# Two stacked window-attention blocks on one core: the bias and mask table moved from a TensorE product to a ScalarE copy, and the query and key products split into high and low parts

## What is computed

```python
h = roll(layernorm(x), (-3, -3)) cut into windows of 7x7 = 49 tokens
q, k, v = h @ qkv_w + qkv_b, per head
attn = softmax((q * hd**-0.5) @ k.T + rel_bias[head] + mask[window])
x = x + roll(windows_back(attn @ v @ proj_w + proj_b), (3, 3))
x = x + gelu(layernorm(x) @ fc1_w + fc1_b) @ fc2_w + fc2_b
```

## Time and profile before

| | |
|---|---|
| median of 3 runs | 7130.31 us |
| time of the profiled execution | 7130.83 us |
| its span in the trace | 7129.1 us |
| granted TensorE clock over the span | 0.997 |
| TensorE busy | 98% |
| VectorE, ScalarE, GpSimd busy | 71%, 66%, 63% |
| mean busy share of the 16 DMA engines | 0.18 |

### The profile page before, as it was taken

The page is one execution under the profiler, slowest core; times in us unless marked ns, Lnnn a source line. Parts: engine busy times, 40 slices in busy tenths (PEclk is TensorE's granted clock), DMA queues, the critical chain, the costliest instruction groups (busy, mean ns, idle before and its releaser), DMA issues.

```text
span 7129.1 us, 284978 instructions
## 1 busy us (share of the span) xinstructions
PE 6951.3 (98%) x98848; PEld 5895.1 (83%) x98848; DVE 5031.9 (71%) x18727; ACT 4674.0 (66%) x9220; POOL 4523.6 (63%) x4612
## 2 busy tenths in 40 slices
PE   6999999999999999999999999999999999999999
PEld 5888888888888888888888888888888888888887
DVE  5777777777777777777777777777777777777775
ACT  3666666666666666666666666666666666666665
POOL 3666666666666666666666666666666666666665
PEclk9999999999999999999999999999999999999999
DMA  1111111111111111111111111111111111111111
GB/s 49 47 46 46 46 46 45 46 45 46 45 46 45 46 45 46 45 47 45 47 45 47 45 47 45 47 44 47 44 48 44 48 44 48 43 48 43 48 43 37
DMA packets 604563, 325.43 MB, mean 46 GB/s; under 512 B 450142, under 2 KB 604128, under 8 KB 604320
## 3 DMA queue, kind: packets, MB, share of 16 engines
q1 hardware_dynamic: 604528, 324.96, 17.5%
HBM read 80.71 MB, written 38.54 MB: 17 GB/s over the span
## 4 chain that ended last, share of the span: by engine, by line
POOL 30%; PE 27%; issue 24%; DVE 17%; POOLq 1%; DVEq 0%; SPq 0%; DMA 0%; ACT 0%
POOL hid_sq L956 8%; POOL x_biased L947 7%; PE ps L422 5%; PE ps L526 5%; PE ps L430 5%; POOL hid_ss L958 4%; POOL rstd L967 4%; POOL rstdM L928 4%; PE ps_o L503 3%; PE ps L515 3%; POOL rstdA L928 3%; DVE x_next L890 3%; DVE bnA L801 2%; DVE bnM L801 2%; DVE o_norm L841 2%
## 5 line engine op out<-in xcount | busy, mean ns | idle before, releaser
L928 POOL TENSOR_TENSOR rstdM<-var_epsM,minus_half 98x4 f32<-98x4 f32 x512 | 515.4, 1007 | 1292.6 <-DVE var_epsM L809 1292.6
L830 DVE TENSOR_TENSOR shifted<-ps,negmax 113x392 f32<-113x392 f32 x2048 | 1161.4, 567 | 213.2
L669 ACT ACTIVATE probsT<-ps 98x392 f32<-98x392 f32 x2048 | 952.3, 491 | 431.3 <-PE ps L483 419.7
L928 POOL TENSOR_TENSOR rstdA<-var_epsA,minus_half 98x4 f32<-98x4 f32 x512 | 518.0, 1012 | 1100.0 <-DVE var_epsA L809 1100.0
L826 DVE TENSOR_REDUCE negmax<-ps 113x8 f32<-113x392 f32 x2048 | 1142.7, 558 | 56.4 <-PE ps L471 28.1
L686 ACT ACTIVATE hid<-ps,bfc 128x392 f32<-128x392 f32 x1536 | 873.0, 587 | 416.3 <-PE ps L542 399.2
L662 ACT ACTIVATE probs<-shifted 113x392 f32<-113x392 f32 x2048 | 997.7, 526 | 23.5 <-DVE shifted L830 15.2
L483 PE MATMUL ps<-ident,probs 113*98 113x113 f32 x8192 | 990.7, 264 | 9.2 <-ACT probs L662 7.7
L503 PEld LDWEIGHTS ps_o<-vM,probsT 98*49 98x49 f32 x32768 | 793.8, 125 | 195.6 <-DVE o_norm L841 128.2
L503 PE MATMUL ps_o<-vM,probsT 98*49 98x50 f32 (+1 forms) x32768 | 851.4, 201 | 78.9 <-DVE o_norm L841 78.7
L483 PEld LDWEIGHTS ps<-ident,probs 113*98 113x98 f32 x8192 | 800.9, 129 | 52.8 <-ACT probs L662 9.6
(11 more groups left out here) (99 smaller groups left out, 15077.7 us busy)
## 6 DMA issues: line engine op xcount, KB each, us to landing
kM<-kT SPq DMA_DIRECT2D x512, 85.8 KB
vM<-vA SPq DMA_DIRECT2D x1024, 41.3 KB
vM<-vA SPq DMA_DIRECT2D x1024, 38.3 KB
x_in<-in_x SPq DMA_DIRECT2D x256, 147.0 KB
x_again<-in_x SPq DMA_DIRECT2D x256, 147.0 KB
kM<-kT SPq DMA_DIRECT2D x1024, 36.8 KB
x_keep<-x_next SPq DMA_DIRECT2D x256, 147.0 KB
out_y<-y_out SPq DMA_DIRECT2D x256, 147.0 KB
```

The costliest lines, as they stand in the source:

```text
L669: act.activation(probsT[:, unit_buffer(L, u), :, :, :], free(ps[bank_of[f"T{L}{u}"]][0:PT, 0:1], (SP, 4), (64, 2), (1, TOK)), ACT.Copy).th ...
L830: dve.tensor_tensor(shifted[:, buf, :].rearrange("p (h k) -> p h k", k=TOK), s, free(negmax[:, buf, 0:1], (1, 8), (0, TOK)), ALU.add).then ...
L928: pool.tensor_tensor(rstd[n][:, :], var_eps[n][:, :], minus_half[:, :], ALU.pow).then_inc(s_rstd[n], 1)
```

## The change

The table: `tleft`, `t_high`, `tlow` and the product L462 go. `table` becomes a plain float32 array of 113 rows that holds bias plus mask for every unit, and a new step of ScalarE, `seed`, copies a unit's part of it into the bank (8 a turn). The scores add onto what ScalarE wrote. For that the places of a bank must count as written by TensorE: only the first matmul of a group that fills a bank starts afresh, three groups are padded from 384 to 392 columns (`PAD` = 8, in `project` and block 1's `fc2`), all banks are filled once at the start, and `scores` of block 0 opens with one matmul of a single column that adds zero.

Queries and keys: `turned` of an A norm now makes two copies on ScalarE, `xqT_high` (float32r) and `xnT`; a new step of VectorE, `low_part_qk`, makes `xqT_low`; `q` and `k` are three float32r products each (`three`, which `fc1` uses too), and their high and low weights are made once at the start.

The orders of all five engines and `BANKS` are new, and LAST is 5: block 0's MLP now works on s2, block 1's attention from the scores on s3, its first MLP part on s4 and its last on s5. `turn` is the same instruction as `pe.transpose`, with other start and stop flags.

```diff
@@ scores @@
-                for u in units:
-                    if free_from := bank_free(x, f"sc{L}{u}"):
-                        pe.wait_ge(*free_from)
-                    if u == units[-1]:
-                        pe.wait_ge(s_qe[L], x.count(1, 1))
-                        pe.wait_ge(s_km[L], x.count(16 * VARIANTS[L], 16 * VARIANTS[L]))
-                    pe.matmul(ps[bank_of[f"sc{L}{u}"]][0:SP, 0:UNIT_COLS], tleft[:, :], table_of(x, L, u),
-                              start=True, stop=False, skip_group_check=True)
+                pe.wait_ge(s_qe[L], x.count(1, 1))
+                pe.wait_ge(s_km[L], x.count(16 * VARIANTS[L], 16 * VARIANTS[L]))
+                pe.wait_ge(s_sd[L], x.count(UNITS[L], units[-1] + 1))
+                if L == 0:
+
+                    pe.matmul(ps[bank_of["sc00"]][0:1, 0:1], ident[:, 1:2], ident[:, 0:1], start=False, stop=True, skip_group_check=True)
@@ scalar @@
+            def seed(x, L, u):
+
+                if x.exists(ns):
+                    if free_from := bank_free(x, f"sc{L}{u}"):
+                        act.wait_ge(*free_from)
+                    act.activation(ps[bank_of[f"sc{L}{u}"]][0:SP, 0:UNIT_COLS], table_of(x, L, u), ACT.Copy).then_inc(s_sd[L], 1)
@@ turned @@
+                    act.activation(xqT_high[L][0:C, :], g, ACT.Copy).then_inc(s_xh[L], 1)
                     act.activation(xnT[L][0:C, :], g, ACT.Copy).then_inc(s_xe[n], 1)
@@ tensor @@
+            def three(out, w_high, w_low, x_high, x_low, low_ready):
+
+                pe.matmul(out, w_high, x_high, start=True, stop=False)
+                pe.matmul(out, w_low, x_high, start=False, stop=False)
+                pe.wait_ge(*low_ready)
+                return pe.matmul(out, w_high, x_low, start=False, stop=True)
@@ q (k alike) @@
-                    pe.wait_ge(s_xe[f"A{L}"], x.count(1, 1))
+                    pe.wait_ge(s_xh[L], x.count(1, 1))
-                    pe.matmul(ps[bank_of[f"q{L}"]][0:QK[L], 0:ST], wqkv[L][:, 0:QK[L]], xnT[L][:, :], start=True, stop=True)\
-                      .then_inc(s_q[L], 1)
+                    three(ps[bank_of[f"q{L}"]][0:QK[L], 0:ST], wqk_high[L][:, 0:QK[L]], wqk_low[L][:, 0:QK[L]],
+                          xqT_high[L][:, :], xqT_low[L][:, :], (s_ql[L], x.count(1, 1))).then_inc(s_q[L], 1)
@@ vector @@
+            def low_part_qk(x, L):
+
+                if x.exists(ns):
+                    dve.wait_ge(s_xe[f"A{L}"], x.count(1, 1))
...
+                    dve.tensor_tensor(xqT_low[L][0:C, :], ps[bank_of[f"xtA{L}"]][0:C, 0:ST], xqT_high[L][0:C, :].bitcast(f32),
+                                      ALU.subtract).then_inc(s_ql[L], 1)
```

More of the change, by code:

```diff
@@ L45, in shape_constants @@
     k = {"ident": np.eye(128, dtype=np.float32)}
[L48 to L58, removed]
+    masks = []
     for last_row in (0, 1):
@@ L62, in shape_constants @@
                 first, pairs, _, heads = unit_place(L, u)
-                block = np.zeros((NREG, pairs, heads, TOK), np.float32)
+                block = np.zeros((SP, pairs, heads, TOK), np.float32)
                 for p in range(pairs):
[L65 to L73, removed]
+                    other_row = rr[:, None] != rr if last_row else np.zeros((TOK, TOK), bool)
+                    other = other_row | (rc[:, None] != rc) if first + p == PAIRS - 1 else other_row
+                    block[HALF[0]:HALF[0] + TOK, p] = -100.0 * other_row[:, None]
+                    block[HALF[1]:HALF[1] + TOK, p] = -100.0 * other[:, None]
+                masks.append(block.reshape(SP, -1))
+    k["mask"] = np.concatenate(masks, 1)
     return k
@@ L404, in _, with turn @@
             pe.wait_ge(s_brow, 32)
+            for bank in ps[:7]:
+                mm = pe.matmul(bank[:, 0:4 * SP], ident[:, :], free(ident[:, 0:1], (0, 4), (1, SP)), start=True, stop=True)
+            mm.then_inc(s_wps, 1)
+            def turn(out, x, first, last):
+                rows = x.ap[0][1]
+                return pe.matmul(out, x, ident[0:rows, 0:rows], start=first, stop=last, is_transpose=True, skip_group_check=True)
             def xT(x, n):
@@ L557, in fc2 @@
                     for c in range(HCH):
-                        w = wfc2[:, c, :] if L == 0 else par128[1][:, P128["fc2"] + C * c:P128["fc2"] + C * (c + 1)]
-                        mm = pe.matmul(g[0:PT, p * step:p * step + width], hid[L][:, c, t], w, start=(c == 0), stop=(c == HCH - 1))
+                        if L == 1 and p == PAIRS - 1 and c == HCH - 1:
+                            width = C + PAD
+                        w = wfc2[:, c, :] if L == 0 else par128[1][:, P128["fc2"] + C * c:P128["fc2"] + C * c + width]
+                        mm = pe.matmul(g[0:PT, p * step:p * step + width], hid[L][:, c, t], w, start=(p == c == 0), stop=(c == HCH - 1),
+                                       skip_group_check=True)
                     if L == 0:
@@ L654, in v_out, with table_of @@
                        .then_inc(s_ve[L], 1)
+            def table_of(x, L, u):
+                col = UNIT_COLS * unit_buffer(L, u)
+                if x.known:
+                    start = (1 if x.i - x.off >= last_row_from else 0) * NT + col
+                    return table[:, start:start + UNIT_COLS]
+                which = (x.i + (256 - last_row_from - x.off)) // 256
+                return table[:, bass.ds(which * NT + col, UNIT_COLS)]
+            def seed(x, L, u):
[3 more added lines that the diff above has]
+                    act.activation(ps[bank_of[f"sc{L}{u}"]][0:SP, 0:UNIT_COLS], table_of(x, L, u), ACT.Copy).then_inc(s_sd[L], 1)
             def exps(x, L, u):
@@ L690, in body @@
                 s0, s1, s2, s3, s4 = Strip(i, 0), Strip(i, 1), Strip(i, 2), Strip(i, 3), Strip(i, 4)
+                gelu(s2, 0, 0)
+                gelu(s2, 0, 1)
+                gelu(s2, 0, 2)
+                seed(s3, 1, 4)
+                seed(s3, 1, 5)
+                exps(s3, 1, 0)
+                probsT_out(s3, 1, 0)
+                exps(s3, 1, 1)
+                exps(s1, 0, 0)
+                exps(s3, 1, 2)
+                turned(s0, "A0")
+                exps(s3, 1, 3)
+                exps(s3, 1, 4)
@@ L726, in _ @@
+                q_out(s0, 0)
+                k_out(s2, 1)
+                gelu(s4, 1, 0)
+                q_out(s2, 1)
+                gelu(s4, 1, 1)
+                seed(s2, 1, 0)
+                seed(s2, 1, 1)
+                seed(s2, 1, 2)
+                turned(s1, "M0")
+                v_out(s0, 0)
+                gelu(s4, 1, 2)
+                v_out(s2, 1)
+                seed(s2, 1, 3)
             iterate(act, body)
@@ L895, in body @@
             def body(i):
[L896 removed]
+                s0, s1, s2, s3, s4, s5 = Strip(i, 0), Strip(i, 1), Strip(i, 2), Strip(i, 3), Strip(i, 4), Strip(i, 5)
                 stats(s0, "A0")
+                low_part(s2, 0)
+                shift(s3, 1, 0)
+                shift(s3, 1, 1)
+                shift(s3, 1, 2)
+                stats(s4, "M1")
+                finish1(s5)
+                shift(s3, 1, 3)
+                shift(s3, 1, 4)
+                shift(s3, 1, 5)
                 third_stats(s2)
[L899 removed]
+                low_part_qk(s0, 0)
                 finish0(s2)
```

236 lines of the change are left out of this document (104 added, 132 removed), and 12 rows, old and new, of the table BANKS.

## The result

The changed kernel takes 7067.72 us, the median of 4 runs (7063.67 to 7070.04). The kernel before took 7129.89 in the same session. The ratio is 0.991, 95% interval 0.990 to 0.993: faster, by 0.9% instead of the 3.1% predicted.

What follows compares the result with a forecast made beforehand. The prediction took TensorE to bound the kernel, with a VectorE chain close behind; after the change, the keys' landing ends a 26.45 us turn. 256 turns (6771) plus 135 give a 6906 us span, time 6907 us, range 6690 to 7050.

Steps and rivals of the forecast that it cites:

- the turn: One pass of the steady loop, 256 in all: 26.45 us, ended by the landing of block 1's keys; chance 0.5.
- the walk: Step-by-step timing of a new turn across the engines: TensorE ready at 25.8 us, the keys there at 26.45.
- 135: Setup, filling and draining outside the 256 turns: 115 us as before plus 20 for the change.
- SyncE's three fixed issues: On SyncE's queue, load_residual, the next turn's load and block 1's key DMAs follow each other; keys there at 26.45 us.
- the 24.4 us of the walk: TensorE's work in a new turn if nothing waited: 26.5 - 1.85 - 0.4 + 0.1 us.
- the forecast's 26.5: TensorE's work in a 27.4 us turn of the kernel before, counted from group start to group start.
- The idle time ahead of attend of block 0: Expected sign on TensorE: an idle stretch of 0.3 us there, ended by o_norm.
- (1): The key DMAs are not last; shifts, ps_o and TensorE set a 25.8 us turn: 6690 to 6800 us; chance 0.23.
- (2): The order hides nearly everything and TensorE is the bound again: a 24.8 us turn, 6484 us; chance 0.06.
- (3): Smaller delays add on the same chain, up to 0.6 us: a 27.0 us turn, 7050 us; chance 0.13 up to 7115.
- (4): ScalarE's seeds make the kernel slower from 0.9 us each; at 1.0 us each the time is 7330 us; chance 0.05.
- no drain: ScalarE's table loads: 1.28 us each, without the skill's 1.38 us drain, which would add some 130 us to the forecast.

Runs made afterwards that it cites:

- e1: The changed kernel with its two 113-row start loads (bias table and mask) each cut into 112 rows and 1 row: 6927.1 us, 0.971 of the kernel before.
- e9: e1 plus one 64 KB DMA of ident, into a buffer nothing reads, ahead of block 1's key DMAs on SyncE: 7072.6 us, 0.991 of the kernel before.
- e12: e10 with finish1 ahead of the middle statistic (M1) on VectorE instead of behind it: 6921.3 us, 0.970 of the kernel before.
- e6: e1 with each seed made by ScalarE in four pieces of 98 columns: 7241.9 us, 1.015 of the kernel before.
- e10: e4 with one VectorE statistic, A0 of the next strip, moved behind the shift and low part of block (1,0): 6848.3 us, 0.960 of the kernel before.
- e4: e1 with SyncE's list reordered so that block 1's key DMAs follow block 0's at once: 6922.6 us, 0.971 of the kernel before.
- e3: e1 with SyncE's keep(s3) put ahead of block 1's key DMAs: 8763.5 us, 1.229 of the kernel before.
- e8: e4 with two VectorE statistics moved: A0 of the next strip behind normalise(1,0), M1 to the end of the turn before: 7059.3 us, 0.989 of the kernel before.

## Why the prediction was wrong in the sum and right in the turn

- **The step that failed** is a term of the sum: "One more turn of pipeline, a larger table to load and the matmuls that fill seven banks at the start come to it; bounded by nothing ... and by one turn and a half, 40 us, I take 20". It was 173 us. 138 of them (287.9 - 150.3) are the two loads with 113 rows; the other 35 are the rest of that sentence and lie inside its bounds. I gave the larger table no price of its own, and the bound of 40 us came from no row. Its bytes would not have found the miss: 1.6 MB more at the 239 GB/s of the start before are 7 us, and e1, with all the bytes, does wait only 6 us longer than the kernel before (28.9 to 22.8). What the walk lacked is that the loads of 98 rows became loads of 113, and that 113 rows go at 26 GB/s. With 135 replaced by 287.9 the same walk gives 7060 us, 0.1% from the measured time.
- The Trainium skill, DMA: Bandwidth & Descriptors, "Why a DMA increments its semaphore by 16 and not by 1", says that a DMA is spread over the largest number of engines up to 16 that divides the size of the slowest dimension of both its patterns: 113 is prime, so one engine; 106 gives two, 112 sixteen. The traces agree: a share of 0.06 and 26 GB/s with 113 rows, 0.12 and 53 GB/s between 40 and 50 us with 106. By that rule the prediction could have had the term.
- **The turn**, 26.45 predicted, 26.485 measured. The keys did end last and SyncE's three fixed issues stood in a row as walked; e9 shows that a delay of them is paid nearly whole. But it was not the forecast's clear margin. I had TensorE ready at 25.8 with 0.5 to 0.7 us of idle time; it was ready at 26.3, with 0.18 of wait and another chain, VectorE's statistic and low part, 0.12 behind. I had read VectorE as ready in time for the next turn and did not see the statistic that opens its turn. Since all three lay within 0.3 us of each other, the number came out right; that it did so to 0.04 us is partly luck.
- **TensorE's work** was more than the 24.4 us of the walk, which went by starts; its busy time, 25.72, is another measure and covers part of each wait. In the kernel before, attend of block 0 starts 0.57 us behind the matmul ahead of it, where that kind follow each other at 0.08, but only 0.32 shows as idle; so the forecast's 26.5 there does not contradict the 26.99 of busy time. By starts, the changed kernel loses about 0.48 ahead of 3503.99, 0.42 ahead of 3513.16, and 0.18 and 0.12 at the end of the turn, 1.2 in all, which leaves some 25.3 of work, an estimate: 0.9 over the walk. About 0.5 of it is what was not saved: by busy time the table products gave 1.49 instead of 1.85 and the split 0.25 instead of 0.4. The rest, 0.4 to 0.5, is work that the new order has more (by busy time, 26.99 - 1.49 - 0.25 = 25.25 against 25.72). Which handovers hold it was not tried.
- The idle time ahead of attend of block 0 was there (0.26 us), but ended by the turned probabilities, not by o_norm; e12 shows how near o_norm stands.
- **The rivals.** (1), TensorE setting the turn at 25.8, did not happen: TensorE arrived later and the keys held. (2) was out of reach, since work alone is about 25.3. (3), small delays, is where the time lay, but for a wrong reason: the turn had none of them. (4): a seed takes 0.49 us (mean 494 ns, two in 0.92), near the Exp of the earlier trace rows, but e6 shows that its threshold of 0.9 was too high and its mechanism not the one that bites: at 0.70 a seed the kernel is 1.5% slower than before, with ScalarE 85% busy, because TensorE waits for late seeds. (By the forecast's own sum 27.33 us a turn is also the point of no change, not that of 0.2% slower.) The table load took 1.28 us with the next Exp 0.01 us behind it, so no drain here either.
- What the change consists of, by e1's neighbours: the seeds 1.0 us a turn, the split 0.28, together 1.28, while the turn fell by 0.92. If the two add up, which no run tested, all the rest of the change, the new order above all, costs about 0.36 us a turn; e10's order gives 0.32 of that back.

## What to carry to other kernels

Look at the number of rows of every load that a change touches, and not at its bytes alone, at the start too: on a kernel of 7 ms two loads with a prime number of rows took away two thirds of the gain of a rebuilt loop, and cutting each in two brought it back. When several chains end within a few tenths of a microsecond, shortening one can give nothing (e4), and the second step the whole (e10); so look at the distance between two groups on the bounding engine and compare it with the smallest one seen, since the trace names a wait only when it is long. And before a step is moved ahead of others on a queue, find what it waits for itself: e3, e8 and e12 each moved a wait to a worse place.

## What was not expected of the hardware

- A load of 113 rows moves 26 GB/s with a busy share of 0.06, one of 106 rows 53 GB/s with 0.12; the same bytes as 112 rows and 1 let the first product start at 28.9 us instead of 169.5. Later loads in the same queue are held up at their issue too (80.58 us for two).
- A wait of 4.6 us in each turn brought TensorE's granted clock to 0.86 on the mean; the products behind it were 0.33 us apart instead of 0.18.
- ScalarE writes 113 x 392 float32 from SBUF into a bank in 494 ns and a quarter of it in 240 ns: by the two sizes, 240 - (494 - 240)/3 = 155 ns of a duration are fixed, an estimate. In a row they overlap, and nine instructions more for the same elements cost 0.83 us (2.11 in e6, 1.28 in e1), 92 ns each.
